# Attention logits of a fused transformer block on TensorE: stationary weights stored octet by octet, one operand repeated by DMA and masked by VectorE

## The reference

```
logits = einsum('bhdi,bhdj->bhij', q, k) + einsum('bhdi,dij->bhij', q, rpe_k) + einsum('bhdi,dij->bhij', k, rpe_q)
attn = softmax(logits, axis=3)
out = einsum('bhij,bhdj->bhdi', attn, v) + einsum('bhij,dij->bhdi', attn, rpe_v)
```

## Time and profile before

| | us |
|---|---|
| median of 3 runs | 3876.37 (3875.5 to 3880.21) |
| the profiled execution | 3886.44 |
| its span, first to last instruction | 3884.6 |
| TensorE busy | 3481.7 (90%) |
| VectorE busy | 2225.5 (57%) |
| ScalarE busy | 1810.0 (47%) |
| GpSimd busy | 1190.5 (31%) |

### The profile page before, as it was taken

The page is one execution under the profiler, slowest core; times in us unless marked ns, Lnnn a source line. Parts: engine busy times, 40 slices in busy tenths (PEclk is TensorE's granted clock), DMA queues, the critical chain, the costliest instruction groups (busy, mean ns, idle before and its releaser), DMA issues.

```text
span 3884.6 us, 66340 instructions
## 1 busy us (share of the span) xinstructions
PE 3481.7 (90%) x22496; PEld 2907.9 (75%) x22496; DVE 2225.5 (57%) x4469; ACT 1810.0 (47%) x2931; POOL 1190.5 (31%) x1192
## 2 busy tenths in 40 slices
PE   4776899999999999999999999999999999999998
PEld 3665777777777777777777777777777777787776
DVE  6884455555555555555555555555555555555554
ACT  6882244444444444444444444444444444444445
POOL 0000133332233333332233333223333333223335
PEclk9997899999999999999999999999999999999999
DMA  7761000000000000000000000000000000000000
GB/s 191 152 147 34 8 10 9 5 6 9 9 7 9 9 9 9 5 6 9 9 7 9 9 9 8 6 7 9 7 9 9 9 9 8 6 7 9 7 8 5
DMA packets 165392, 79.34 MB, mean 20 GB/s; under 512 B 81631, under 2 KB 163871, under 8 KB 165023
## 3 DMA queue, kind: packets, MB, share of 16 engines
q1 hardware_dynamic: 162946, 72.99, 9.0%
q10 hardware_dynamic: 2416, 5.97, 0.5%
HBM read 60.65 MB, written 14.97 MB: 19 GB/s over the span
## 4 chain that ended last, share of the span: by engine, by line
issue 56%; POOL 21%; PE 10%; DVE 2%; SPq 1%; ACT 1%; POOLq 1%; DMA 0%; ACTq 0%; DVEq 0%
POOL gelu L908 20%; PE bank L434 3%; PE bank L510 1%; PE bank L475 1%; PE bank L463 1%; POOL gst L921 1%; PE bank L533 1%; PE bank L534 1%; PE bank L469 1%; PE bank L443 1%; SPq L393 1%; POOLq L907 1%; ACT gelu L842 1%; PE bank L447 1%; PE bank L444 1%
## 5 line engine op out<-in xcount | busy, mean ns | idle before, releaser
L908 POOL TENSOR_TENSOR gelu<-gelu 128x386 f32<-128x386 f32 x1024 | 1031.0, 1015 | 2116.6 <-ACT gelu L842 2110.2
L841 ACT ACTIVATE gelu<-bank,b_s 128x386 f32<-128x386 f32 x1024 | 595.6, 582 | 1334.4 <-DVE gelu L626 1328.2
L434 PE MATMUL bank<-gelu,w_s 128*128 128x386 f32 x2048 | 832.5, 493 | 31.8 <-POOL gelu L908 28.5
L626 DVE TENSOR_TENSOR gelu<-bank,ratio 128x386 f32<-128x386 f32 x1024 | 564.1, 555 | 465.7 <-PE bank L447 459.9
L842 ACT ACTIVATE gelu<-gelu,b_s 128x386 f32<-128x386 f32 x1024 | 623.6, 609 | 0.0
L443 PE MATMUL bank<-x_hi,w_hi 128*128 128x386 f32 x1024 | 523.5, 511 | 51.5 <-ACT gelu L841 47.7
L533 PE MATMUL bank<-k_f,q_bd 128*128 128x193 f32 x1600 | 510.5, 401 | 48.4 <-DMA a_bd<-u_scratch 48.4
L533 PEld LDWEIGHTS bank<-k_f,q_bd 128*128 128x128 f32 x1600 | 463.4, 332 | 69.8 <-DMA a_bd<-u_scratch 39.8
L534 PE MATMUL bank<-rw,a_bd 128*128 128x193 f32 x1600 | 514.0, 403 | 0.0
L727 DVE TENSOR_REDUCE mx<-bank 128x2 f32<-128x386 f32 (+1 forms) x416 | 226.0, 543 | 456.0 <-PE bank L534 456.0
L534 PEld LDWEIGHTS bank<-rw,a_bd 128*128 128x128 f32 x1600 | 460.4, 336 | 0.0
(11 more groups left out here) (146 smaller groups left out, 4901.4 us busy)
## 6 DMA issues: line engine op xcount, KB each, us to landing
xt<-in_x SPq DMA_DIRECT2D x192, 196.0 KB
q_bd<-q_f SPq DMA_DIRECT2D x512, 6.2 KB
a_bd<-u_scratch SPq DMA_DIRECT2D x256, 25.0 KB, 2.2
txt_s<-in_txt SPq DMA_DIRECT2D x32, 128.0 KB, 2.2
rv<-in_rel_v ACTq DMA_DIRECT2D x1, 3200.0 KB, 18.7
u_scratch<-k_f SPq DMA_DIRECT2D x32, 100.0 KB, 2.2
u_scratch<-q_f SPq DMA_DIRECT2D x32, 100.0 KB, 2.2
out<-o_s SPq DMA_DIRECT2D x64, 48.5 KB
```

Source lines behind the costliest of these rows:

```text
L434: mm(yb[:, 0:T2], w2_s[:, f, :], gelu1[:, f % RING, :], start=(f == 0), stop=(f == NF - 1)).then_inc(S["w2_done"], 1)
L626: v.tensor_tensor(gelu2[:, f % RING, :], zb[f % 2][:, 0:T2], ratio[:, :], ALU.mult).then_inc(S["z2_done"], 1)
L841: a(gelu1[:, f % RING, :], zb[f % 2][:, 0:T2], ACT.Gelu, bias=b1_s[:, f:f + 1]).then_inc(S["g_done"], 1)
L908: g.tensor_tensor(gelu1[:, f % RING, :], gelu1[:, f % RING, :], gelu2[:, f % RING, :], ALU.add).then_inc(S["hs_done"], 1)
```

## The change

An octet becomes 8 neighbouring query rows (8o to 8o + 7), and the weights are stored octet by octet, so each 128-column weight slice is one run in memory. The 16 DMAs of q stay 16, but each now writes 25 runs of 8 elements (32 bytes) in each of its 8 partitions. The relative part is no longer cut to the diagonal by DMA: 8 DMAs copy all 200 columns of `u_scratch` for all 16 combinations into a new tile `a_rep`, contiguous in each partition, and VectorE multiplies it with a 0/1 mask into `a_bd`, in four steps `am0` to `am3` of 7, 6, 6 and 6 octets. These stand in the order between the expert chunks ahead of `log0`. `log0` on TensorE waits for the masking instead of the DMAs. The tables `rw` (193 + 24 to 385 columns) and `rv` (6400 to 5248 columns) are laid out for the new rows. The reciprocal and the scaling of the output take 193 neighbouring columns instead of 200 reordered ones.

```diff
-RW = OCT - 1 + L
+RW = 2 * L - 1
-    "c c c c c vt0 hkeep log0 log1 log2 c log3 log4 log5 c log6 log7 c log8 "
+    "c c am0 c am1 c am2 c am3 vt0 hkeep log0 log1 log2 c log3 log4 log5 c log6 log7 c log8 "
-        q_bd = sb("q_bd", [P, BH, LP])
-        a_bd = sb("a_bd", [P, BH, LP])
+        q_bd = sb("q_bd", [P, OCT, BH, 8])
+        a_rep = sb("a_rep", [P, BH, LP])
+        a_bd = sb("a_bd", [P, OCT, BH, 8])
-                    sp.dma_start(q_bd[rows, bh, :], q_f[rows, :]).then_inc(S["q_spread"], 16)
+                    sp.dma_start(q_bd[rows, :, bh, :], q_f[rows, :].rearrange("p (o r) -> p o r", r=8)).then_inc(S["q_spread"], 16)
-                    sp.dma_start(a_bd[r:P - 7 + r:8, :, OCT * r:OCT * r + OCT],
-                                 u_scratch[:, :, :, OCT * r:OCT * r + OCT].rearrange("b s d i -> (s d) b i")).then_inc(S["a_spread"], 16)
+                    sp.dma_start(a_rep[r:P - 7 + r:8, :, :], u_scratch[:, :, :, :].rearrange("b s d i -> (s d) b i")).then_inc(S["a_spread"], 16)
-                        pe.wait_ge(S["a_spread"], t * N_AS + N_AS)
+                        pe.wait_ge(S["a_masked"], t * 4 + 4)
-                        mm(dst, q_bd[:, :, o::OCT], k_f[:, 0:L], start=True, stop=False)
-                        m = mm(dst, a_bd[:, :, o::OCT], rw[:, OCT - 1 - o:OCT - 1 - o + L], start=False, stop=True)
+                        mm(dst, q_bd[:, o, :, :], k_f[:, 0:L], start=True, stop=False)
+                        m = mm(dst, a_bd[:, o, :, :], rw[:, 192 - 8 * o:192 - 8 * o + L], start=False, stop=True)
-                v.reciprocal(rows(t2, b), by_row(pv[b], 256)).then_inc(S["rec_done"], 1)
+                v.reciprocal(t2[:, b * LP:b * LP + L], pv[b][:, 256:256 + L]).then_inc(S["rec_done"], 1)
+                elif s[:2] == "am":
+                    o0, o1 = (0, 7, 13, 19, OCT)[int(s[2]):int(s[2]) + 2]
+                    if s == "am0":
+                        dve.wait_ge(S["a_spread"], t * N_AS + N_AS)
+                    v.tensor_tensor(a_bd[:, o0:o1, :, :],
+                                    a_rep[:, :, 8 * o0:8 * o1].rearrange("p b (o r) -> p o b r", r=8),
+                                    K["mask_q"].unsqueeze(1).unsqueeze(1).broadcast_to([P, o1 - o0, BH, 8]),
+                                    ALU.mult).then_inc(S["a_masked"], 1)
-            for x in (q_bd, a_bd):
-                g.memset(x[:, :, :], 0.0).then_inc(S["setup_pool"], 1)
+            g.memset(q_bd[:, :, :, :], 0.0).then_inc(S["setup_pool"], 1)
```

More of the change, by code:

```diff
@@ L72 @@
 _at = 0
-for _n, _w in (("ident", P), ("ones", P), ("g8", P), ("g4", P), ("mask_r", 8), ("place", HD + HD + HD)):
+for _n, _w in (("ident", P), ("ones", P), ("g8", P), ("g4", P), ("mask_r", 8), ("mask_q", 8), ("place", HD + HD + HD)):
     CO[_n] = (_at, _w)
@@ L117, in resident @@
         b2_s=sb("b2_s", [P, E]),
-        rv=sb("rv", [P, 2 * OCT * P]),
+        rv=sb("rv", [P, (LP + P) * HD]),
         w2_s=sb("w2_s", [P, NF, P]),
@@ L214, in _ @@
             for r in range(8):
-                c0 = 294 - OCT * r
+                c0 = 126 - r
                 act.dma_start(R["rw"][r:P - 7 + r:8, :], a["rel_rev"][:, c0:c0 + RW]).then_inc(R["const_in"], 16)
@@ L323, in fused_block @@
         names = """w1_in w1_hi_ready w1_split setup_dve setup_pool setup_act tok_in txt_t h_ready qk_ready v_ready
-            bn mv_ready gmean gspread gvar gve grstd affine_part affine norm q_spread a_spread u_out log_ready max_done log_done
+            bn mv_ready gmean gspread gvar gve grstd affine_part affine norm q_spread a_spread a_masked u_out log_ready max_done log_done
             vt v_copied exp_done tr_ready tr0_copied tr1_copied wm_done pv_done pv_ready rec_done o_part obn omv omean ospread ovar ove orstd oaff_part oaffine
@@ L335, in fused_block @@
         V2 = lambda t: t[:, 0:T2]
-        rv_o = rv[:, :].rearrange("p (c o m) -> p c o m", c=2, o=OCT)
-        by_row = lambda ps, a: ps[:, a:a + LP].rearrange("p (o r) -> p r o", r=8)
-        rows = lambda t, b: t[:, b * LP:(b + 1) * LP].rearrange("p (r o) -> p r o", r=8)
         block = ctx.enter_context(nc.Block())
@@ L410, in _ @@
                 sp.wait_ge(S["h_ready"], t * 2 + 2)
-                tokens(t + 1, lambda: sp.wait_ge(S["log_ready"], t * FILLS) if t else sp.wait_ge(S["setup_pool"], 2))
+                tokens(t + 1, lambda: sp.wait_ge(S["log_ready"], t * FILLS) if t else sp.wait_ge(S["setup_pool"], 1))
                 spread(t)
@@ L576, in attend @@
                         part = pv[g % 2][:, (o - octs[0]) * P:(o - octs[0] + 1) * P]
-                        mm(part, rv_o[:, 0, o, :], pr[0][:, o, :, :], start=True, stop=False)
-                        m = mm(part, rv_o[0:JC[1][1], 1, o, :], pr[1][0:JC[1][1], o, :, :],
+                        mm(part, rv[:, (8 * o + P) * HD:(8 * o + P) * HD + P], pr[0][:, o, :, :], start=True, stop=False)
+                        m = mm(part, rv[0:JC[1][1], 8 * o * HD:8 * o * HD + P], pr[1][0:JC[1][1], o, :, :],
                                start=False, stop=True)
@@ L752, in attend @@
                     dve.wait_ge(S["rec_done"], t * 2 + b + 1)
-                    v.tensor_tensor(rows(t1, b), by_row(pv[b], 0), rows(t2, b), ALU.mult).then_inc(S["o_part"], 1)
+                    v.tensor_tensor(t1[:, bs], pv[b][:, 0:L], t2[:, bs], ALU.mult).then_inc(S["o_part"], 1)
                     dve.wait_ge(S["o_part"], t * 2 + b + 1)
@@ L964, in shape_constants @@
     put("mask_r", p[:, None] // HD == np.arange(8)[None])
+    put("mask_q", p[:, None] % 8 == np.arange(8)[None])
     w = np.zeros((P, 3 * HD))
@@ L984 @@
     rel = i["L0_attn_rel_emb"]
-    j_of = np.arange(P)[:, None, None, None] + P * np.arange(2)[:, None, None]
-    rel_rows = np.maximum(OCT * np.arange(8)[:, None] + np.arange(OCT) - j_of + L - 1, 0)
     arrays = {
@@ L993 @@
         "gn_in": np.stack(gn_columns(i["L0_attn_gn_qkv_scale"]) + gn_columns(i["L0_attn_gn_qkv_bias"]), 1),
-        "rel_rev": rel[0:HD, ::-1], "rel_v": rel[HD:2 * HD].T[rel_rows].transpose(0, 1, 3, 2, 4).reshape(P, -1),
+        "rel_rev": rel[0:HD, ::-1], "rel_v": rel[HD:2 * HD].T[np.maximum(np.arange(LP + P)[None] - np.arange(P)[:, None] + 64, 0)].reshape(P, -1),
         "gn_out": np.stack([i["L0_attn_gn_out_scale"], i["L0_attn_gn_out_bias"]], 1),
```

## The result

The changed kernel takes 4032.8 us (median of 4 runs, 4032.3 to 4034.2) against 3878.3: a ratio of 1.040 with a 95% interval of 1.038 to 1.042, slower, 154 us more. The forecast was 3958 (3850 to 4045). The sign and the chain of causes came as told. The profiled execution took 4032.3 us, its span 4030.5. That of the kernel before was 8 us longer than its median, so a turn's difference between the two traces is a little smaller than between the medians.

The account below looks back on a forecast made before the run. TensorE, busy 90% of the span, was taken to set the pace. Per turn 8.1 - 7.0 + 1.7 - 0.1 = +2.7 us, in all +83 on 3876.4, gave 3959, rounded to 3958 us (range 3850 to 4045).

Parts of the forecast that it names:

- The sign: Whole kernel: the change makes it slower, given a chance of 0.73.
- chain of causes: Each turn: faster weight loads shorten the logits, but VectorE waits for copies, TensorE for gelus and masks; clock falls.
- Weights in one run: Logit stage on TensorE: weight slices without the 100-byte step load faster, gaining 7.0 us a turn (6.5 to 7.7).
- The exchange of the two banks: Logit stage: VectorE's emptying of banks becomes late next, taking 0.6 us off the gain, 1.2 at the lower end.
- The DMAs of q: SyncE's queue: still 16, 200 runs cost no more to issue; 0 us, bounds -0.5 and +2.
- The copies: DMAs into a_rep: 1.64 MB instead of 0.2, 6.6 us of traffic (5.2 to 8.7), last landing at 1987.8.
- The sentence on the ports: Copies into a_rep: every eighth partition reaches half of 16 ports, traffic 7.5 us, sum 0.9 a turn higher; not adopted.
- The wait on VectorE: Ahead of log0: am0 waits for the copies, then masks and scalings take 6.4 us; log0 8.1 later (6.2 to 11).
- the term that decides: VectorE's wait for the copies moves forward to am0, behind the second chunk, holding up later chunks; log0 loses 8.1 us.
- The clock: TensorE idles ahead of log0, so its clock drops to the lower level: 1.7 us a turn lost (0 to 3.4).
- second idle time: TensorE idle again for some 2 us ahead of log0, after about 7 us waiting for chunk 3's gelu.
- Smaller edits: Reciprocal over 193 instead of 200 columns gains 0.1 us a turn; smaller memset and tables gain 1 us once.

Follow-up runs that it names:

- e1: The kernel before, only with each weight slice of q_bd and a_bd read as 128 neighbouring elements (logits not the reference's): 3689 us, 0.954.
- e11: The changed kernel with each of the 8 copies filling 16 neighbouring partitions of a_rep instead of every eighth: 4197 us, 1.083.
- e7: The changed kernel with u_scratch laid out in long runs and one DMA instead of 8 filling a_rep, same bytes: 4004 us, 1.033.
- e3: The changed kernel with am0 to am3 moved behind the five chunks, vt0 and hkeep, right ahead of log0: 4051 us, 1.045.
- e4: The changed kernel with SyncE's queue reordered: 3 q DMAs, the 8 copies into a_rep, then the other 13 q DMAs: 3807 us, 0.982.
- e2: The changed kernel with the 8 copies into a_rep carrying 25 of the 200 columns each: 3916 us, 1.010.
- e12: The changed kernel with filler products on TensorE: 24 ahead of its fifth chunk, 6 behind the logits: 3996 us, 1.031.
- e9: e8 plus 6 filler products while TensorE waits for ScalarE's copy of the probabilities behind the logits: 3690 us, 0.952.
- e8: The changed kernel with one long-run copy issued behind the third q DMA, and each logit step waiting only for its own masks: 3719 us, 0.959.
- e10: e8 without the 16 q DMAs; VectorE makes q_bd by multiplying q_f with a 0/1 mask in four steps: 3785 us, 0.977.

## Why the prediction was right, and where its sizes were off

The chain of causes is there as forecast: loads of 194 ns, a logit stage of 21 us, VectorE waiting for the copies and TensorE for VectorE's gelus, VectorE busy 133 us more (128 forecast), the mean clock down to 0.938. The size is nearly twice the forecast, near the upper end of the range; that it stayed inside owes something to masks and clock costing less than the forecast had.

- *Weights in one run.* Forecast 7.0 a turn (6.5 to 7.7). e1 has 6.5, and in the changed kernel it is 6.2, with 0.3 of it lost to the clock. The exchange of the two banks took all of its 1.2 us, not 0.6: in the row at 2063.69 of the same stage the third logit step waits for the bank.
- *The DMAs of q.* Taken as 0; the 16 took 11.89 us instead of 10.95, 0.9 a turn, inside the bound of 2. 200 runs of 32 bytes do show in the issue, by 0.06 us a DMA.
- *The copies.* This is the step that was most mis-sized. Forecast: landing 8.6 us behind the first issue (2.2 + 6.6 would be 8.8, a slip of 0.2); measured 10.5 on average. I put the traffic at 6.6 us, between the issue's 5.2 and 8.7 at the 188 GB/s of the earlier trace rows. The window under e11 shows 203 GB/s while the copies run, so 8.1 us: the upper end, from the row of the busiest stretch, was the near one. The sentence on the ports in the prediction (7.5 us, an estimate by the Trainium skill, "SBUF — State Buffer", section "Door 1: The DMA port swizzle") leaned the right way: 16 x 800-byte runs into every eighth partition reach 8 of 16 ports by that page. e11, in other partitions, agrees that the place written matters (119 against 203 GB/s). e7, which writes all 128 partitions and goes at 196, does not fit a rate set by the ports alone; what limits it is open.
- *The wait on VectorE.* Forecast 6.4 us from landing to log0; measured 5.6. The masks took 1.09, 0.95, 0.95 and 1.29, against 1.10 and 0.97 worked out from the earlier trace rows; only the last began beside a running sum of GpSimd, for 0.3 instead of 0.6. The total, log0 10.2 us later, was 8.1 in the forecast (bounds 6.2 to 11). The prediction calls the wait's early place the term that decides. It doesn't: moved behind the chunks (e3) it gives back 1.8 of the 10.2, and the clock takes that again. What decides is when the copies land, by their place in SyncE's queue (e4) and their bytes (e2).
- *The clock.* Forecast 1.7 a turn. e12 measures 1.1, of which up to 0.4 is lost before the change too (before, turns with a low stretch behind the logits have a rest of 64.4 us or more, the others 62.8). The low clock lasts 10.2 us in most turns, longer than in the earlier trace rows, but 9.3 of 11.6 us lie ahead of log0. There TensorE mostly waits; it also makes the products of the fifth chunk at the low clock, from 2057.32 on, but these fit under the masks, since log0 still waits 0.24 us for am3 in the row at 2060.60. The prediction's second idle time of some 2 us ahead of log0 is that 0.24. The Trainium skill, "TensorE: Matmul & The Clock Gate", section "HAM oscillation — how this bites in real kernels", has the clock go down in every round in which a wait for data comes; the trace agrees: in each of the 13 turns a low stretch of 6.8 or 10.2 us begins ahead of log0. What it costs depends on what stands behind the gap (e3 against the changed kernel).
- *Smaller edits.* The reciprocal is 1360 ns instead of 1398; as forecast.

The sum was 8.1 - 7.0 + 1.7 - 0.1 = 2.7; measured 10.2 - 6.5 + 1.1 - 0.1 = 4.7, as the three parts of the table have it. (With the clock at 0.7, net of what the kernel before loses, 0.4 of it would have no term.) Between the medians the difference is 5.0 a turn. Of the 2.0 between forecast and trace, 1.9 are the copies, 0.9 the issue of the q DMAs, 0.5 the logits; the masks (-0.8) and the clock (-0.6) go the other way.

## What to carry to other kernels

Stationary weights read with a step of 100 bytes made each load 1.77 times as long (332 against 188 ns), and the loads set the pace of these products. Storing the weights in one run is worth it, but only where the rearrangement finishes before TensorE arrives. When a transfer grows, ask first where it stands in its queue and how many bytes go to which partitions, and only then who waits for it: with the copies behind 16 small DMAs the change was 4.0% slower; ahead of 13 of them, with nothing else changed, it was 1.8% faster (e4); and with one copy, a wait per octet and one filler as well, 4.8% (e9). A gap that can't be closed costs least where the low clock behind it falls into waiting time, and most ahead of the densest stretch.

## What the runs showed of the hardware

- A DMA copy of 1.64 MB in 128 runs of 12.8 KB landed in 9.9 us, and in 2048 runs of 800 bytes in 10.5; into groups of 16 neighbouring partitions it took 15.6.
- A small gap of TensorE can cost more than a large one. With 24 products in the 9 us gap of the changed kernel the mean clock rose to 0.973 and the time stayed; 6 products in a gap of 1.8 us, in e9, won 29 us. A low stretch of 3.4 us in the stream behind the logits makes a turn 1.6 us longer or more (64.4 against 62.8 in the trace of the kernel before).
- SyncE's issue of small DMAs is held up behind a large one: 13 q DMAs took 9.8 us behind eight copies (e4) and 14.0 behind one large copy (e8), where a single issue took 4.9.
- A VectorE product with both inputs in SBUF takes 0.95 us for 768 elements when no sum of GpSimd runs as it begins, and 1.28 to 1.5 when one does (a_bd in e4, e8 and e10); the sums beside it take up to 1.9 us instead of 1.0. In e10 the masks into q_bd took only 0.94 to 1.03 near the same sums; why isn't known.
